# Causal mask in spare contraction rows, a cap of one in the weighing, and exponentials by pairs of heads in a fused graph-attention, Mamba-2, relational and expert kernel

## The reference

```python
cs = jnp.cumsum(a, axis=-1)
ss = cs[..., :, None] - cs[..., None, :]
mask = jnp.tril(jnp.ones((T, T), dtype=bool))
return jnp.where(mask, ss, -jnp.inf)            # segsum
...
Lmat = jnp.exp(segsum(dA))
xdt = xh * dtc[..., None]
Y_diag = jnp.einsum('bcln,bcsn,bhcls,bcshp->bclhp', Cc, Bc, Lmat, xdt)
```

## Time and profile before

| | |
|---|---|
| median of 3 runs | 3507.71 us (3505.94 to 3511.50) |
| the profiled execution | 3515.14 us, its span 3513.2 us |
| PE busy in the span | 3396.7 us (97%) |
| DVE, ACT, POOL busy | 2532.4, 1723.9, 1788.3 us (72%, 49%, 51%) |
| mean granted TensorE clock | 0.987 of 2.4 GHz |
| rounds | up to about 2460 us; 73.2 us for two in the steady part |
| expert phase | the rest, over 1000 us |

### The profile page before, as it was taken

One profiled execution on the slowest core, in us unless ns is written; L12 is line 12 of the kernel. 1 busy time (PEld: TensorE's weight loads), 2 busy tenths in 40 slices (PEclk: granted clock), 3 DMA queues, 4 the chain that ended last, 5 costly groups with the idle time before them and its releaser, 6 DMA issues.

```text
span 3513.2 us, 62394 instructions
## 1 busy us (share of the span) xinstructions
PE 3396.7 (97%) x19338; PEld 2783.3 (79%) x19338; DVE 2532.4 (72%) x7349; ACT 1723.9 (49%) x3690; POOL 1788.3 (51%) x2043
## 2 busy tenths in 40 slices
PE   7999999999999999999999999997799999999998
PEld 6777777777777777777777777776688888888887
DVE  4888888888888888888888888886344444444444
ACT  3655655655655665655656556554233322333322
POOL 2455455555455555455555555554455554555553
PEclk8999999999999999999999999999899999999999
DMA  3111111111111111111111111110455555556653
GB/s 124 40 37 52 39 36 51 39 36 51 39 36 45 45 36 50 40 36 51 39 42 48 36 51 39 38 50 22 143 194 199 192 192 198 191 192 200 194 191 129
DMA packets 168166, 304.67 MB, mean 87 GB/s; under 512 B 38000, under 2 KB 140400, under 8 KB 149936
## 3 DMA queue, kind: packets, MB, share of 16 engines
q0 software_dynamic: 38272, 196.98, 16.4%
q1 hardware_dynamic: 92880, 72.41, 7.2%
q10 hardware_dynamic: 36960, 34.62, 3.4%
HBM read 250.77 MB, written 53.17 MB: 87 GB/s over the span
## 4 chain that ended last, share of the span: by engine, by line
PE 91%; issue 3%; DVE 3%; ACT 1%; POOL 1%; another core or an unknown queue 1%; DMA 1%; ACTq 0%; DVEq 0%; SPq 0%; POOLq 0%
PE bank L1165 14%; PE bank L1437 14%; PE bank L1451 14%; PE bank L1181 12%; PE bank L1282 7%; PE bank L1396 6%; PE bank L1381 5%; PE bank L1174 4%; PE bank L1363 3%; PE bank L1313 2%; PE bank L1235 2%; PE bank L1304 1%; DVE x L1004 1%; PE bank L1209 1%; PE bank L1403 1%
## 5 line engine op out<-in xcount | busy, mean ns | idle before, releaser
L767 ACT ACTIVATE decay<-bank,w_up 128x256 f32<-128x256 f32 x568 | 268.8, 473 | 701.2 <-PE bank L1437 695.4
L1165 PE MATMUL bank<-xn1T,w_in 128*128 128x256 f32 x2304 | 524.0, 382 | 7.0 <-issue 5.9
L1181 PE MATMUL bank<-w_rel,hT 128*128 128x264 f32 x2048 | 523.5, 394 | 0.0
L1437 PE MATMUL bank<-zs,w_up 128*128 128x256 f32 x2272 | 504.9, 381 | 0.6 <-ACT zs L623 0.6
L1451 PE MATMUL bank<-w_dn,decay 128*128 128x256 f32 x2272 | 502.1, 379 | 0.0
L1165 PEld LDWEIGHTS bank<-xn1T,w_in 128*128 128x128 f32 x2304 | 432.6, 190 | 65.6 <-issue 9.4
L1437 PEld LDWEIGHTS bank<-zs,w_up 128*128 128x128 f32 x2272 | 433.6, 191 | 60.4 <-issue 0.9
L1451 PEld LDWEIGHTS bank<-w_dn,decay 128*128 128x128 f32 x2272 | 426.2, 190 | 55.1
L1113 DVE TENSOR_TENSOR hT<-bank,w_dn 128x256 f32<-128x256 f32 x142 | 60.2, 424 | 537.0 <-PE bank L1451 537.0
L847 DVE SCALAR_TENSOR_TENSOR conv<-bank,conv_w,conv 128x255 f32<-128x255 f32 (+2 forms) x960 | 425.9, 477 | 20.8
L1181 PEld LDWEIGHTS bank<-w_rel,hT 128*128 128x128 f32 x2048 | 364.0, 190 | 80.0 <-issue 24.2
(11 more groups left out here) (238 smaller groups left out, 6166.0 us busy)
## 6 DMA issues: line engine op xcount, KB each, us to landing
token_rows<-row SPq DMA_DIRECT2D x64, 266.0 KB, 3.0
xT_sb<-in_xT ACTq DMA_DIRECT2D x64, 256.0 KB
x_sb<-in_x ACTq DMA_DIRECT2D x64, 256.0 KB, 3.0
adj_sb<-in_adj SPq DMA_DIRECT2D x64, 256.0 KB, 3.5
adjt_sb<-in_adjT SPq DMA_DIRECT2D x64, 256.0 KB, 3.6
out<-row SPq DMA_DIRECT2D x64, 256.0 KB, 2.4
w_in<-token_rows,idc POOLq DMA_INDIRECT x142
out<-hT,ids POOLq DMA_INDIRECT x142
```

The source lines that it names most:

```text
L767: nc.scalar.activation(hid(f), bank[f % 4][:, 0:GROUP], ACT.Relu, bias=b1[q % 2][:, f:f + 1]).then_inc(hid_ready, 1)
L1165: ins = mm(dst, w_in[:, k, first:first + P], xn1T[:, k, :], start=k == 0, stop=k == DK - 1)
L1181: ins = mm(bank[6 + t][:, 0:GX], hT[:, d, r * N + t * P:r * N + (t + 1) * P], w_rel[:, r, d, :], start=r == 0 and d == 0, stop=r == R - 1 ...
L1437: ins = mm(bank[f % 4][:, 0:GROUP], w1[i][:, k, f * P:(f + 1) * P], xgT[:, k, :], start=k == 0, stop=k == DK - 1)
```

## The change

- `negmask` and `identb` go, and with them the mask products of line 1209. `expo` begins with the products of cs[l], whose first now starts the bank, and contracts over all 32 rows of a quadrant.
- The rows of a quadrant that no head uses get constants at the start of the program: there the cumulative sum runs with `factors` in place of ones and begins at 1, and `selneg` holds a multiple of -2^60 in columns left of a row's mark. The marks are 4 columns apart, so that this mask is a staircase. What it leaves above the diagonal is handled next.
- `weigh` is `min(decay, 1) * g`, one scalar_tensor_tensor of the same 768 columns in place of a tensor_tensor, and g is 0 above the diagonal: DVE makes g from its bank by a product with `causal` (400 columns). ACT's copy of g goes.
- ACT takes the exponentials of two heads at once, 768 columns over two neighbouring banks; `EXPO` becomes (2, 3, 4, 5), g moves to bank 3 and the transposed x to banks 4 and 5. `expo` waits by pairs.
- ACT's two copies of 8 columns into x become one.

```diff
@@ setup, POOL
-            gp.memset(negmask[:], 0.0)
-            gp.memset(identb[:], 0.0)
+            gp.memset(causal[:], 1.0)
...
+            gp.iota(place_no, [[0, T], [1, P]], base=0, channel_multiplier=0, allow_small_or_imprecise_dtypes=True)
@@ setup, DVE
+            v.tensor_copy(mark[:], row_mark[:])
...
+                v.tensor_scalar(selneg[:, u, 0:P], marked, mine_neg[:, u:u + 1], None, ALU.add)
+                v.tensor_scalar(selneg[:, u, P:N], ones_row[:, P:N], mine_neg[:, u:u + 1], None, ALU.mult)
+            v.tensor_scalar(factors[:], factors[:], 1.0, None, ALU.max).then_inc(rows_named, 1)
@@ ACT
+            def exponentials(j, b):
+                act.wait_ge(expo_made, 8 * b + 2 * j + 2)
+                if j == 0:
+                    need(act, y_made, 2 * b)
+                nc.scalar.activation(decay[:, 2 * j:2 * j + 2, :], expo_banks[j % 2][:, :, 0:TRI],
+                                     ACT.Exp).then_inc(decay_ready, 1)
...
-                    for t in range(T):
-                        copy(x[:, t, D:GX], bank[t][:, GX + 2:WS])
+                    copy(x[:, :, D:GX], banks[:, 0:T, GX + 2:WS])
...
-                if b2_ is not None:
-                    act.wait_ge(g_made, b2_ + 1)
-                    need(act, m_ready, 4 * b2_)
-                    copy(g[:], bank[5][:, 0:TRI + T * H]).then_inc(g_ready, 1)
...
-                    for h in range(H):
-                        act.wait_ge(expo_made, 8 * b2_ + h + 1)
-                        if h == 0:
-                            need(act, y_made, 2 * b2_)
-                        nc.scalar.activation(decay[:, h, :], bank[EXPO[h % 4]][:, 0:TRI], ACT.Exp).then_inc(decay_ready, 1)
+                    for j in range(H // 2):
+                        exponentials(j, b2_)
@@ DVE
-                    dve.wait_ge(decay_ready, 8 * b + 2 * j + 2)
-                    v.tensor_tensor(decay[:, 2 * j:2 * j + 2, :], decay[:, 2 * j:2 * j + 2, :],
-                                    g[:, 0:TRI].unsqueeze(1).broadcast_to([P, 2, TRI]), ALU.mult).then_inc(m_ready, 1)
+                    dve.wait_ge(decay_ready, 4 * b + j + 1)
+                    v.scalar_tensor_tensor(decay[:, 2 * j:2 * j + 2, :], decay[:, 2 * j:2 * j + 2, :], 1.0,
+                                           g[:, 0:TRI].unsqueeze(1).broadcast_to([P, 2, TRI]), ALU.min,
+                                           ALU.mult).then_inc(m_ready, 1)
...
-                    ch2.link(dve, v.tensor_tensor_scan(cs[:], ones_row[:], dA[:], 0.0, ALU.mult, ALU.add), b2_)
+                    ch2.link(dve, v.tensor_tensor_scan(cs[:], factors[:], dA[:], 1.0, ALU.mult, ALU.add), b2_)
...
                 if b2_ is not None:
+                    dve.wait_ge(g_made, b2_ + 1)
+                    v.tensor_tensor(g[:], bank[3][:, 0:GW], causal[:], ALU.mult).then_inc(g_ready, 1)
                     dve.wait_ge(g_ready, b2_ + 1)
@@ PE, expo
-                    else:
-                        pe.wait_ge(decay_ready, 8 * b + h - 3)
-                    mm(bank[EXPO[h % 4]][:, :].rearrange("p (s l) -> p s l", s=T)[:, :, 0:P], identb[:],
-                       negmask[:].unsqueeze(1).broadcast_to([P, T, P]), start=True, stop=True)
+                    elif h % 2 == 0:
+                        pe.wait_ge(decay_ready, 4 * b + h // 2 - 1)
+                    q, u = h % 4, h // 4
+                    mm(bank[EXPO[q]][:, 0:N], sel[32 * q:32 * q + 32, u, :], cs3[32 * q:32 * q + 32, :],
+                       start=True, stop=False, skip_group_check=True)
...
```

More of the change, by code:

```diff
@@ L97, in sem @@
             return ctx.enter_context(nc.semaphore(name))
-        bank = [ctx.enter_context(nc.psum_tensor(f"bank{i}", [P, 512], F32)) for i in range(6)]
-        bank67 = ctx.enter_context(nc.psum_tensor("bank67", [P, 2, 512], F32))
-        bank += [bank67[:, i, :] for i in range(2)]
+        banks = ctx.enter_context(nc.psum_tensor("bank", [P, 8, 512], F32))
+        bank = [banks[:, i, :] for i in range(8)]
         rows_d = nc.dram_tensor("token_rows", [NT, ROW], F32, kind="Internal").ap()
@@ L292, in graph_mamba_moe @@
         che, chp = Chain(sem("dve_expert"), 5), Chain(sem("dve_plan"), 10)
+        expo_banks = banks[:, 2:4, :], banks[:, 4:6, :]
         def by_tile(a):
@@ new lines, in _ @@
+            v.tensor_tensor(used[:], mine[:, 0:1], mine[:, 1:2], ALU.add).then_inc(rows_named, 1)
+            dve.wait_ge(rows_named, 4)
+            v.tensor_scalar(minus_used[:], used[:], -1.0, None, ALU.mult)
+            v.tensor_scalar(spare[:], used[:], -1.0, 1.0, ALU.mult, ALU.add).then_inc(rows_named, 1)
+            dve.wait_ge(rows_named, 5)
+            carry(dve)
+            v.tensor_scalar(less_hi[:], row_part[:], 1.0, minus_used[:], ALU.is_ge, ALU.mult)
+            v.tensor_scalar(less_mid[:], row_part[:], 2.0, minus_used[:], ALU.is_ge, ALU.mult)
@@ new lines, in _ @@
+            v.tensor_scalar(first_mark[:], mark[:], 0.0, spare[:], ALU.is_equal, ALU.mult)
+            v.tensor_scalar(raise_by[:], spare[:], 1.0 / TINY, None, ALU.mult)
+            v.tensor_scalar(low[:], spare[:], TINY, None, ALU.mult)
+            v.tensor_scalar(mask_by[:], spare[:], MASKED, None, ALU.mult).then_inc(rows_named, 1)
+            dve.wait_ge(rows_named, 6)
+            carry(dve)
+            v.tensor_tensor(again[:], used[:], first_mark[:], ALU.add)
+            v.tensor_scalar(marked, place_no[:, 0:P], mark[:], mask_by[:], ALU.is_lt, ALU.mult)
@@ L1028, in step @@
                     need(dve, rows_out, 16 * b3_)
-                    ins = v.tensor_tensor(row[:, :, 0:GX], bank67[:, :, 0:GX], x2b[:], ALU.add)
+                    ins = v.tensor_tensor(row[:, :, 0:GX], banks[:, 6:8, 0:GX], x2b[:], ALU.add)
                     ins.then_inc(x3_ready, 1)
@@ L1206, in expo @@
                         pe.wait_ge(xdt_ready, 2 * b + h - 1)
[L1207 to L1210 removed]
+                    elif h % 2 == 0:
[3 more added lines that the diff above has]
+                       start=True, stop=False, skip_group_check=True)
+                for h in heads:
+                    q, u = h % 4, h // 4
+                    mm(bank[EXPO[q]][:, N:TRI], sel[32 * q:32 * q + 32, u, :], cs3[32 * q:32 * q + 32, P:N],
+                       start=False, stop=False, skip_group_check=True)
                 for first, width, s, l in ((0, N, 0, 0), (N, TRI - N, P, P)):
@@ L1213, in expo @@
                         q, u = h % 4, h // 4
-                        mm(bank[EXPO[q]][:, first:first + width], sel[32 * q:32 * q + 3 * H, u, :],
-                           cs3[32 * q:32 * q + 3 * H, l:N], start=False, stop=False, skip_group_check=True)
-                for first, width, s, l in ((0, N, 0, 0), (N, TRI - N, P, P)):
-                    for h in heads:
-                        q, u = h % 4, h // 4
-                        ins = mm(bank[EXPO[q]][:, first:first + width], cs3[32 * q:32 * q + 3 * H, s:s + P],
-                                 selneg[32 * q:32 * q + 3 * H, u, 0:width], start=False, stop=True,
+                        ins = mm(bank[EXPO[q]][:, first:first + width], cs3[32 * q:32 * q + 32, s:s + P],
+                                 selneg[32 * q:32 * q + 32, u, 0:width], start=False, stop=True,
                                  skip_group_check=True)
```

56 lines of the change are left out of this document (34 added, 22 removed).

## The result

The change made the kernel slower. It took **3588.1 us** (median of 4 runs, 3585.8 to 3594.3) against 3508.4 for the kernel before (4 runs): a ratio of 1.0223, 95% interval 1.0211 to 1.0236, or 80 us more. Forecast were 3496 us, with 3480 to 3514 as the range and 0.14 for slower.

A forecast was written before the change was run, and what follows sets the result against it. Two chains bound it: DVE up to the slot round's x1, then PE from line 1174 to the next T. 11.6 us from 29 pairs, plus 2.6, minus 2, made 12 us: 3507.7 to 3496, range 3480 to 3514.

The forecast's parts named there:

- the last of the change's parts: DVE's set-up: some 25 more small instructions, under 3 us, covered by a wait of 3.98 us, so no cost.
- D: Rival, chance 0.13: POOL's masks hold two more weighings in DVE's chain, or weighings run slower; 14 us slower, 3522.
- the forecast of 72.8: Sign that the forecast is right: two rounds take 0.40 us less, 72.8 us in place of 73.20.
- First group hidden on PE, its gain by way of the exponentials: Mask products before line 1363: PE gains nothing; first weighing 0.45 us earlier, 1.36 us after T, end of turned probabilities.
- Exponentials by pairs: ACT: 768 columns take 0.80 us where two single exponentials took 0.88.
- Second group: Mask products before line 1174: route round gains 0.44 us, PE's arrival and x1 from DVE agreeing on it.
- g on DVE: DVE's product for g, 400 columns: 571 ns, adding 0.05 us to its chain in the slot round.
- The cap: Weighing by scalar_tensor_tensor with the minimum, 768 columns on DVE: no change in time.
- A: Rival, chance 0.26: route round's second weighing falls behind a POOL mask, DVE pays 0.44 us; no change, 3507.
- B: Rival, chance 0.10: slot round's weighing gets in front of the mask, each pair wins another 0.44 us; 3483.
- The sum, 0.40 us per pair: Slot round's x1, and with it line 1174, comes 0.45 - 0.05 = 0.40 us earlier per pair of rounds.
- The total: Whole run: 29 pairs give 11.6 us, first and last rounds 2.6, broken rounds -2; 12 us, 3496.

The follow-up runs named there:

- with 32 more: Changed kernel plus 32 tiny idle memsets in DVE's set-up, ahead of its first wait: 3480.9 us, ratio 0.9925 to the kernel before.
- with 25 more: Kernel before plus 25 idle memsets in front of DVE's first wait, nothing of the change: 3594.0 us, ratio 1.0247.
- zeros in the first group: Changed kernel plus 32 memsets, mask products of heads 0 to 3 put back each round as products of zeros: 3501.0 us, ratio 0.9978.
- g twice: Changed kernel plus 32 memsets, DVE making the product of causal mask into g a second time, into an unread tile: 3505.4 us, ratio 0.9964.
- with 14 more: Changed kernel plus 14 tiny idle set-up instructions on DVE: 3500.8 us, ratio 0.9958.
- single exponentials: Changed kernel plus 32 memsets, ACT's exponentials one head at a time again in place of pairs: 3477.4 us, ratio 0.9903.
- the split: Changed kernel plus 32 memsets, DVE's last two slot instructions moved ahead of the variance of the output projection: 3466.5 us, ratio 0.9860.
- the slots later: Changed kernel plus 32 memsets, all ten of DVE's slot instructions moved behind the scaling of xn1, before the wait for Y: 3511.7 us, ratio 1.0003.

## Why the prediction was wrong

**The step that failed is the last of the change's parts**: "The setup has some 25 more small instructions on DVE, under 3 us, in front of a wait of 3.98 us, which covers them." In time they were covered, as the same instruction in the set-up of the change shows: it starts at 10.72 us (11.06 before), and 0.50 us of the wait is left.

```profile
10.72 0.24 DVE L833 SCALAR_TENSOR_TENSOR w_gc<-bank,gate_w 128x8 f32<-128x8 f32 x2 [0.50 <-PE bank L1176]
```

What they cost is their place. The set-up got 20 more by the records, and 5 products for g came in behind it; together they moved the loop by 25 instructions, to where its 281 lie on four blocks of code. The prediction had put the price of that at nothing. It is some 105 us (ratio 1.0223 against 0.9925 with 32 idle ones more), 3.9 us for each of 27 turns, and it alone turns a gain into a loss. No rival had it, D included; D's place, DVE's chain, was the right one, its cause was not.

One more term could hide in these 3.9 us. The changed kernel shows a mean granted clock of 0.980 where the kernel before shows 0.987: in 15 of 25 steady turns TensorE's clock falls to 1.2 GHz for 3.4 us, shortly behind the stop that left it idle; with 32 more this happens once in all the rounds. It costs little here: the 15 turns take 77.22 us in the median, the ten others 77.05. On the kernel before with 25 more the two kinds differ by more, 77.66 against 76.39, still far less than the stop.

**The rest, read from the versions without the stop.** Intervals are T to T, medians over the steady rounds of one trace. The 73.20 us of the prediction was a window that is not a whole period. From T to T a pair of the kernel before takes 73.74, so the forecast of 72.8 stands for 73.34 here. The window of one such pair of the kernel before reads:

```profile
1532.30:1606.04 73.74, 73.09 (x452) 58.09 (x451) 64.22 (x190) 44.06 (x93) 39.77 (x44) 1.00 0.15 43
```

and that of the change with 32 more:

```profile
1504.88:1578.06 73.18, 71.51 (x438) 56.64 (x442) 65.15 (x192) 42.44 (x81) 39.74 (x44) 1.00 0.15 43
```

- *First group hidden on PE, its gain by way of the exponentials:* right. Weighing at T + 1.36; putting the group back cost 20 us, half of it by the hold of a mask.
- *Exponentials by pairs:* 809 ns each over the trace, 1.51 us for two, so 0.11 of overlap; forecast 0.80 and 0.11. The 826 and 93 that the prediction took from the Trainium skill ("ScalarE: Activation LUTs", What ACT_TABLE_LOAD costs) are further off; taken together they would have put the weighing 0.04 us later, not 0.02, and the sum at 11 us. The pairs are worth 0.07 us in a route round and nothing that the measured times can tell.
- *Second group:* the attention product of the route round 0.45 earlier, as forecast, but I gave the credit to both chains. DVE's alone was enough: with the group put back the pair is the same.
- *g on DVE:* 0.567 us, forecast 0.571. Of the +0.05 us that it was to add, 0.01 shows: the first weighing of the slot round starts at T + 1.82, before at T + 1.81.
- *The cap:* free, 0.95 to 0.96 us a weighing that nothing holds, as before.
- *Rivals A and B, a weighing behind or in front of a mask:* neither came; the second weighing of the route round kept its 0.95, that of the slot round took 1.41 (1.39 before). Both margins moved together, as the forecast had it. The two experiments that moved one of them alone (zeros in the first group, g twice) lost 0.4 us a round by this hold.
- *The sum, 0.40 us per pair:* measured 0.57 (73.75 to 73.18): the route round gained 0.43 and the slot round 0.15. Some 0.12 of the latter is an "issue" gap of TensorE ahead of the projections (0.24 us before, 0.12 after). I had not seen it and did not test why it shrank.
- *The total:* 27 steady pairs give 15 us. The medians say 26 to 28 (ratios 0.9925 and 0.9920), the version with 14 more says 15 (0.9958). The difference is of the size of the odd stops: single rounds 1 to 8 us longer than their like, 23 us in the trace of before, 6 with 32 more, 19 with 14 more, 1 with single exponentials. They differ from run to run of like code. Much of them stands in the waits from 200 to 2300 us as ACT in front of an exponential, for "remote", which is nothing that the profile can name: 24.1 us in 6 waits before, 8.0 in 1 with 32 more, 21.5 in 4 with 14 more, 5.9 in 2 with single exponentials. What makes them stays open, and with it whether more than 15 us of the gain are the change's own. So without the stop the forecast of 12 us (3496) would have been short by some 3 us in the steady rounds and by about 15 in the medians.

## What to carry to other kernels

Before an edit to code ahead of a loop is called free, count the instructions of the loop's body on each engine (from the records between two branches back, waits among them) and see how many blocks of 128 it touches. The sign in a profile is an "issue" wait at the first instruction of the body, once a turn, with more packets on the instruction queue; then shift the loop by a few idle instructions, or make room by shortening the body. And judge a removed product by what waits at the next meeting of the chains, not by its engine's share: of two equal groups, the one that was hidden on its engine cost 20 us when it was put back, the one in the open nothing.

## What the runs showed of the hardware that I had not expected

- One idle instruction more can cost 133 us (16 against 17 on the kernel before, 3510.9 to 3643.8) or save 175 (13 against 14 on the change).
- What the stop costs depends on how many instructions stand ahead of the next edge: 3.64 us with 14, 3.73 and 1.49 with 4, 6.20 in one with 1. Where the branch alone lies in the fourth block it is 5.07 us; there one packet starts at 1750.35 us and the next at 1750.65, both 2 us behind the branch (1748.3), so the fetch of the target starts right behind another one (that this makes the difference was not tested).
- Small DVE instructions wait for POOL too. In slot rounds three of the ten slot instructions (128x4) take 0.47, 0.59 and 0.49 us, the first two while POOL adds x2b, the cast while it makes a mask; all ten take 0.15 to 0.19 us where they stand behind xn1, and the cast 0.16 ahead of the variance. The first two end when an instruction of x2b does: in the slot round above at 1541.46 and 1542.16 us, where x2b's two end at 1541.44 and 1542.14, and by the median over all slot rounds 0.02 us behind it. The Trainium skill ("SBUF — State Buffer", Who interferes with whom) names both kinds as contending with POOL, and calls the shared ports an exclusive lock; the two products agree.
- A long weighing doesn't wait for the whole of a mask (1.5 us). How long it is held depends on how far behind the mask's start it begins: in the median it takes 1.41 us at 0.0 us behind (g twice), 1.19 to 1.24 at 0.2 (the split and the slots later), 1.14 at 0.3 (slots later), and 0.95 to 0.96, as without a mask, from 0.5 on (0.55 in the earlier trace rows). A few lie off this line (seven of the kernel before take 1.36 at 0.2), and why the hold is short was not tested.
